# Graph attention on one core: ACT evicts the head outputs undivided, GpSimd divides a whole graph at once and marks the missing edges

## The reference

```
q, k, v = split_heads(x @ Wq + bq), split_heads(x @ Wk + bk), split_heads(x @ Wv + bv)
scores  = q k^T / sqrt(32) + beta * adj
scores  = where(adj > 0, scores, -9e15)
out     = softmax(scores) @ v                     # heads side by side again: 256 x 384
x       = layernorm(x + out)                      # mean and variance over the 384 columns
```

## Time and profile before

| what | value |
|---|---|
| median of 3 runs | 678.68 us (678.59 to 680.06) |
| profiled execution, own time | 678.75 us |
| its span, first to last instruction | 677.0 us |
| busy: PE, PEld | 635.4, 514.5 us |
| busy: DVE, ACT, POOL | 597.7, 576.0, 406.9 us |
| mean granted PE clock | 0.993 |

### The profile page before, as it was taken

The page is one execution under the profiler, slowest core; times in us unless marked ns, Lnnn a source line. Parts: engine busy times, 40 slices in busy tenths (PEclk is TensorE's granted clock), DMA queues, the critical chain, the costliest instruction groups (busy, mean ns, idle before and its releaser), DMA issues. The chain is left out here.

```text
span 677.0 us, 21340 instructions
## 1 busy us (share of the span) xinstructions
PE 635.4 (94%) x6304; PEld 514.5 (76%) x6304; DVE 597.7 (88%) x2385; ACT 576.0 (85%) x2024; POOL 406.9 (60%) x642
## 2 busy tenths in 40 slices
PE   5899999999999999999999999999999999999981
PEld 5788877787878787878777777888787878787850
DVE  3898899988999898989898989898989998898974
ACT  4799888889898889898888888888989888988881
POOL 3413266766566775566775556676556676566743
PEclk9999999999999999999999999999999999999997
DMA  8065556567656557755557755556765556765441
GB/s 254 4 148 142 139 136 166 126 164 187 172 143 162 137 140 189 185 150 153 145 122 187 187 155 151 153 119 177 188 172 144 154 127 157 189 168 144 114 101 70
DMA packets 68226, 101.93 MB, mean 151 GB/s; under 512 B 10512, under 2 KB 36368, under 8 KB 68112
## 3 DMA queue, kind: packets, MB, share of 16 engines
q1 hardware_dynamic: 67024, 100.37, 57.9%
q10 hardware_dynamic: 1088, 0.20, 0.2%
HBM read 22.94 MB, written 12.58 MB: 52 GB/s over the span
## 5 line engine op out<-in xcount | busy, mean ns | idle before, releaser
L433 ACT ACTIVATE probs<-neg_scores,neg_max 128x256 f32<-128x256 f32 x768 | 382.4, 504 | 4.4 <-DVE neg_max L515 2.9
L515 DVE CUSTOM_DVE_ANT_0 neg_scores<-s_bank,bias_sb 128x256 f32<-128x256 f32 x768 | 282.3, 416 | 54.2 <-ACT probs L433 45.0
L554 DVE STREAM_TRANSPOSE blocks<-probs 128x512 f32<-128x512 f32 x248 | 171.3, 700 | 0.0
L433 ACT ACTIVATION_READ_ACCUMULATOR probs<-neg_scores,neg_max 128x1 f32 x768 | 149.8, 195 | 0.0
L326 PE MATMUL j_bank<-xt_high,w_high 128*128 128x256 f32 x576 | 115.6, 309 | 1.9 <-ACT w_high L465 1.5
L399 PE MATMUL s_bank<-qk 32*128 32x256 f32 x1536 | 110.0, 399 | 5.4 <-DVE neg_max L515 3.7
L399 PEld LDWEIGHTS s_bank<-qk 32*128 32x128 f32 x1536 | 72.6, 184 | 46.7 <-ACT v_sb L452 28.1
L760 POOL TENSOR_SCALAR o_sb<-y_sb,rstd,shift 128x384 f32<-128x384 f32 x60 | 99.3, 1662 | 9.6 <-POOL shift L755 9.6
L326 PE MATMUL j_bank<-xt_high,w_low 128*128 128x256 f32 x576 | 99.5, 280 | 0.0
L326 PE MATMUL j_bank<-xt_low,w_high 128*128 128x256 f32 x576 | 99.2, 280 | 0.0
L369 PE MATMUL j_bank<-ident,probs 128*128 128x128 f32 x544 | 84.1, 278 | 13.9 <-issue 12.8
(11 more groups left out here) (56 smaller groups left out, 899.2 us busy)
## 6 DMA issues: line engine op xcount, KB each, us to landing
shuffled<-blocks SPq DMA_DIRECT2D x496, 128.0 KB, 3.1
x_sb<-in_x_dram SPq DMA_DIRECT2D x32, 384.0 KB, 3.3
out_dram<-o_sb SPq DMA_DIRECT2D x30, 384.0 KB, 4.3
adj_sb<-in_adj_dram SPq DMA_DIRECT2D x32, 256.0 KB, 3.7
out_dram<-o_sb SPq DMA_DIRECT2D x4, 192.0 KB, 2.1
blocks<-in_L_gnn_Wq_dram SPq DMA_DIRECT2D x1, 576.0 KB, 5.8
blocks<-in_L_gnn_Wk_dram SPq DMA_DIRECT2D x1, 576.0 KB, 8.2
blocks<-in_L_gnn_Wv_dram SPq DMA_DIRECT2D x1, 576.0 KB, 9.6
```

The source lines that it names most:

```text
L433: nc.scalar.activation(probs[:, (T * s + t) % (T * NX), :], neg_scores[:, (T * s + t) % (T * NH), :], ACT.Exp, bias=neg_max[:, n % 2, t, h ...
L515: nc.vector.tensor_tensor_reduce(neg_scores[:, (T * s + t) % (T * NH), :], s_bank[h % J][:, t * N:(t + 1) * N], bias_sb[:, n % 2, t, :], - ...
L554: nc.vector.transpose(blocks[:, n % 2, :, h, :, :].rearrange("p k t q -> p t k q"), probs[:, slot:slot + T, :].rearrange("p t (k q) -> p t ...
```

## The change

G jobs of graphs 0 to 29 are taken out by ACT with a plain copy into `att`. DVE keeps only the six G jobs of graphs 30 and 31, and divides those as before. GpSimd gets `divide(n - 2)`, one multiply of the whole 128 x 768 `att` of a graph in place by the reciprocal sums broadcast over 32 columns, ahead of `add_residual(n - 2)`. `edges` is dropped from DVE; its operation is the first one of GpSimd's `bias`. `inv_sum` gets a third buffer. The whole diff, unchanged context left out:

```
     def on_act(job):
-        return job[0] in "QVXO" or (job[0] == "T" and (job[2] < B - 1 or job[1] % 2 == 1))
+        return (job[0] in "QVXO" or (job[0] == "T" and (job[2] < B - 1 or job[1] % 2 == 1))
+                or (job[0] == "G" and job[2] < B - 2))
     def on_dve(job):
-        return job[0] in "KXG" or (job[0] == "T" and not on_act(job))
+        return job[0] in "KX" or (job[0] in "TG" and not on_act(job))
...
-        inv_sum = sb("inv_sum", [P, 2, T, H])
+        inv_sum = sb("inv_sum", [P, 3, T, H])
+        divided = sem("divided")
...  # ACT, take
+                elif kind == "G":
+                    wait(act, y_ready, n - 1)
+                    ins = nc.scalar.activation(att[:, n % 2, :, a * P:(a + 1) * P],
+                                               b[:, 0:N].rearrange("p (t d) -> p t d", t=T), ACT.Identity)
...  # DVE, take of G: inv_sum[:, n % 2, ...] becomes inv_sum[:, n % 3, ...]
             def invert(n, g):
                 dve.wait_ge(exp_ready, T * (H * n + J * (g + 1)))
-                nc.vector.reciprocal(inv_sum[:, n % 2, :, J * g:J * (g + 1)],
+                wait(dve, divided, n - 2)
+                nc.vector.reciprocal(inv_sum[:, n % 3, :, J * g:J * (g + 1)],
                                      row_sum[:, n % 2, :, J * g:J * (g + 1)]).then_inc(inv_ready, 1)
-            def edges(n):
-                dve.wait_ge(adj_in[n % 2], (n // 2 + 1) * DMA)
-                nc.vector.tensor_scalar(bias_sb[:, n % 2, :, :], adj_sb[:, n % 2, :, :], 0.0, MASKED,
-                                        ALU.is_le, ALU.mult).then_inc(not_edge_ready, 1)
...
-            edges(0)
...
-                    if h == 0 and n + 1 < B:
-                        edges(n + 1)
...  # GpSimd
             def bias(n):
                 pool.wait_ge(adj_in[n % 2], (n // 2 + 1) * DMA)
+                wait(pool, max_ready, T * H * (n - 1))
+                nc.gpsimd.tensor_scalar(bias_sb[:, n % 2, :, :], adj_sb[:, n % 2, :, :], 0.0, MASKED,
+                                        ALU.is_le, ALU.mult).then_inc(not_edge_ready, 1)
                 wait(pool, bias_ready, n)
...
+            def divide(n):
+                pool.wait_ge(taken_a, max(act_taken[place["G", g, n] + 1] for g in range(G)))
+                pool.wait_ge(inv_ready, G * (n + 1))
+                heads = att[:, n % 2, :, :].rearrange("p t (h d) -> p t h d", h=H)
+                nc.gpsimd.tensor_tensor(heads, heads, inv_sum[:, n % 3, :, :].unsqueeze(3).to_broadcast([P, T, H, HD]),
+                                        ALU.mult).then_inc(divided, 1)
             def add_residual(n):
-                pool.wait_ge(taken_v, max(dve_taken[place["G", g, n] + 1] for g in range(G)))
+                pool.wait_ge(divided, n + 1)
                 pool.wait_ge(res_ready, n + 1)
...  # the loop over n
                 if n >= 2:
+                    divide(n - 2)
                     add_residual(n - 2)
```

More of the change, by code:

```diff
@@ L544, in take @@
                         b[:, 0:N].rearrange("p (t j d) -> p t j d", t=T, j=J),
-                        inv_sum[:, n % 2, :, J * a:J * (a + 1)].unsqueeze(3).to_broadcast([P, T, J, HD]), ALU.mult)
+                        inv_sum[:, n % 3, :, J * a:J * (a + 1)].unsqueeze(3).to_broadcast([P, T, J, HD]), ALU.mult)
                 ins.then_inc(taken_v, 1)
```

## The result

The changed kernel takes 720.21 us in the median of 4 runs (718.4 to 720.37), against 678.89 for the one before beside it (678.59 to 680.06): 1.060 times as long, 95% interval 1.058 to 1.062. It is slower, by 41 us; forecast were 728, in a range of 700 to 752. The profiled execution took 720.16 us, its span is 718.4.

A forecast was written before the change was run, and what follows sets the result against it. PE bounded the kernel before at 20.08 us a graph; the GpSimd loop, grown to 21.85 us, would bind. Over 28 turns, with the start, 49.0 us on 678.75 gives 727.8, predicted as 728 us, range 700 to 752.

The forecast's parts named there:

- The loop: DVE's moments through GpSimd's bias and y back to DVE: 17.92 us grows to 21.85, against PE's period of 20.08.
- the division: GpSimd's in-place broadcast multiply of 128 x 768: 1.83 us per graph, bounds 1.8 and 3.3.
- the edges: Comparison ahead of line 714 on GpSimd: 2.01 us per graph, bounds 1.3 and 2.2.
- moments to the first operation of the bias: Loop's other half, DVE's moments to GpSimd's next bias: 12.61 us, can't shrink much.
- The sum: Whole run: 28 turns of 21.85 us instead of 20.1, 49.0 us later, giving 727.8 us.
- The start: First bias delayed by the edges: 0.5 us charged, first graph's moments at 75.1 instead of 74.6 us.
- The tail: After the moments of iteration 30: no wait for y in iteration 31, tail as before.
- The clock: PE's granted clock: no change expected, with PE busy about 90% of each graph.
- DVE's relief: G jobs and edges off DVE, 1.58 us a graph: priced at nothing, gain at most 13 us.
- rival B: DVE's relief removes PE's gap at the low part of X, 13 us in all: 666 us; chance 0.05.
- Rival A: Both new GpSimd operations fit in the 2.16 us spare, PE stays the bound: 678 to 681 us; chance 0.04.
- SP's queue: x, adjacency and store come right ahead of the shuffle, which starts some 1.5 us later: no term.

The follow-up runs named there:

- e3: Changed kernel with two Newton steps instead of three in GpSimd's layer norm (the last two graphs keep three); 676.7 us, 0.996 of the kernel before.
- e4: Kernel before the change with five Newton steps instead of three in GpSimd's layer norm; 706.15 us, 1.039 of the kernel before.
- e9: Kernel before the change with four Newton steps instead of three on GpSimd; 679.82 us, 1.001 of the kernel before.
- e10: Changed kernel with four Newton steps instead of three on GpSimd; 763.19 us, 1.123 of the kernel before.
- e1: Changed kernel with the edges back on DVE, G staying on ACT and the division on GpSimd; 669.38 us, 0.985 of the kernel before.
- e2: Kernel before the change with only the edges moved to GpSimd, G and its division staying on DVE; 679.17 us, 1.000 of the kernel before.
- e5: Kernel of e1 with only group 2's G job on ACT, groups 0 and 1 on DVE as plain copies; 671.21 us, 0.988 of the kernel before.
- e11: Changed kernel with DVE's moments moved to head 9 and the seed to head 10; 686.94 us, 1.011 of the kernel before.

## Why the prediction was right

**The loop.** The forecast, that GpSimd's chain from moments to y outgrows PE's period by 1.77 us, was right in place, sign and kind, and the measured excess is 1.4 us (21.55 - 20.11); e3, e4, e9 and e10 show it by its length alone, e1 and e2 by its two new parts. Its terms, forecast and measured in one turn: the division 1.83 and 1.49 us; the edges 2.01 and 1.94; a gap of 0.09 behind the edges (410.37 + 1.94 to 412.40), which I had left out; moments to the first operation of the bias 12.61 and 12.72, most of the difference being another gap of 0.09 in front of the edges (406.98 + 3.30 to 410.37); y to moments 0.1 and 0.03. Together 21.85 and 21.51, in the mean of the 28 turns 21.55.

**The sum.** 28 turns x 0.30 us = 8.5 us too much. The start came out at 74.5 instead of 75.1, 0.6 too much. The tail from the moments of iteration 30 on is 720.16 - 677.79 = 42.4 us, where I took the old 40.9: 1.5 too little. 8.5 + 0.6 - 1.5 = 7.6 us is the distance of 727.8 to the profiled 720.16. The one term that is much mis-sized is the division: a multiply whose second operand is broadcast over its innermost 32 columns is cheaper than the rows 724 and 731 of the same size that I read it from, not dearer, as my upper bound feared. That is also why GpSimd has 105 us more to do and not 120; ACT has 27 more, where 34 were forecast.

**The edges.** The neighbour of the same form was the right row (1.93 in the mean of 32). The Trainium skill's line rate for one-input work on GpSimd (GPSIMD Engine Reference, section 4.1, Engine selection) would have given 683 us by the prediction's sum: the trace disagrees, with 1.93 us for 512 elements where DVE took 0.385. Nor does the branching cost of section 3.1 (Elementwise) show, 5.1 us by the prediction's estimate from that page.

**The clock: wrong.** I expected no change; it fell to 0.50 for some 3.4 us after gaps of 2.0 us, to 0.97 in the mean from 400 to 500 us. That it costs nothing in the turns is shown by e10. It does explain why the profile has 22 waits for y and not some 30. In the eight turns behind a slow stretch DVE comes late itself and waits 0 to 0.45 us, partly too short to be shown (the reciprocal ahead of the moments at 419.16 ends at 419.01, y at 419.13). In the other twenty it waits 1.6 to 1.8 us, and 2.35 in the last. That this is less than the 2 to 5 us forecast has nothing to do with the clock: it is the loop's 21.5 us less the 19.7 that a turn takes in e1, where DVE waits for y only once. The tail's 1.5 us may be the clock's. Most of it (1.3 us) lies between the moments of iterations 30 and 31, where the clock was 0.50 from 682 to 686 us behind a gap of 2.25; e4, with a gap of 1.4 there and the clock at 1.00, has none of it. But the wait for y is shorter in e4 too, so this is not shown.

**DVE's relief: priced at nothing, which came out right in this kernel, but for a false reason.** Against rival B I wrote that the relief lies elsewhere than where PE's wait arises. That was wrong: the G job of group 2 at head 6 stands in a stretch in which DVE has no idle time (from head 4 to head 9), and taking it out shortens PE's wait by 0.25 us a graph (e5). My upper bound of 13 us was also too low, since I took PE's gap as shown, 0.45 us, and the start-to-start distance says 0.6. Rival B was thus right in mechanism and overruled by the loop; in e1, where the loop fits, its gain is 10 us. Rival A had the wrong time for the same reason: a loop that fits lets the relief show, and e1 and e3, whose loops fit, take 669 and 677 us where it had 679.

**SP's queue: no term, right here, with less room than I claimed.** The changed kernel has no wait for the shuffle on PE. That holds as long as moments and y are early enough for the shuffle; e11 is the case where it binds.

## What to carry to other kernels

Before work goes to a half-idle engine, walk its chain of waits once around and compare that length with the period of the engine that bounds: spare time in the loop (2.2 us here), not idle time on the engine (7 us a period), is what can be spent. A relief counts only in the stretch without idle time ahead of a wait of the bounding engine, and such a wait is to be read from start to start against an undisturbed place, not from the gap shown. Lengthening the loop by a few tiny instructions, in both kernels, tells a loop from a load within two runs.

## What was not expected of the hardware

- A GpSimd multiply of 128 x 768 with the innermost 32 columns broadcast takes 1.48 us, against 1.83 to 1.85 for the same size with two full operands or one broadcast over the middle dimension.
- The GpSimd comparison with a multiply (`is_le`, 128 x 512) takes 1.93 us, hardly less than maximum and multiply, 2.02.
- PE's granted clock fell after some gaps of about 2 us and not after others (1.00 behind the gaps of 2.12 us at 99.4 and of 2.01 at 379.5, 0.50 behind that of 2.03 at 401.0). In e4, with gaps of 1.0 to 1.6 us each turn, it stayed at 1.00 from 75 to 675 us. What tells the first cases apart is open.
